# Three rounds of graph layers on one Trainium2 core: another order of sweeps, a fifth bank, splits lowered later, and three fp32r passes in rows that took fp32

## The chip, the cores and the metric

The kernel runs on one core of a Trainium2 chip. The metric is device time in microseconds (us) of one execution, the median over several. The engines are named as in the profile: PE is TensorE (PEld its weight load), DVE is VectorE, ACT is ScalarE, POOL is GpSimd and SP is SyncE, which here only starts transfers.

## The reference, cut to what matters

`adj` is 4096 x 4096, node features are 4096 x 128, and everything is fp32.

```python
def _mlp(x, W1, b1, W2, b2, W3, b3):        # a = leaky_relu, slope 0.01
    x = a(x @ W1 + b1)
    x = a(x @ W2 + b2)
    return a(x @ W3 + b3)

u = x
for _ in range(3):
    v = _mlp(adj @ u, uv_W1, uv_b1, uv_W2, uv_b2, uv_W3, uv_b3)
    u = _mlp(adj @ v, vu_W1, vu_b1, vu_W2, vu_b2, vu_W3, vu_b3)
x = layernorm(x + v)
x = layernorm(x + adj @ (x @ weight))
```

Only the v of the third round is used. So `adj` is multiplied six times, each time with the result of the time before: products 0 to 4 are followed by the three layers, product 4 also by the first normalization, and product 5 by the projection and the second normalization.

## The kernel before, in words

**Splitting.** A product is worked out in three passes of the type fp32r: a tile of `adj` is split into `high` (an ACT copy, L427) and `low` (raw minus `high`, a DVE subtraction, L551), and the operand into `p_high` and `p_low`. The passes are high by `p_low`, high by `p_high`, low by `p_high` (L771).

**Tiles and visits.** The 4096 rows are 8 chunks of 512. A tile holds 512 rows by 256 columns and is 0.5 MB; a chunk of columns is two tiles, loaded together by one transfer of 1 MB. A visit is one tile multiplied into one sum in PSUM: six matmuls. Each product has 128 visits, 768 in all. Where the operands allow, a tile once split is visited for product k and then for product k+1, before it is thrown away (`both`). There are 8 slots for split tiles (`SLOTS`) and four raw buffers of two tiles.

**Sweeps.** Product 0 with 56 visits of product 1 is the first sweep of 184 visits. Sweep k (1 to 4) has 128 visits: the rest of product k, and 56 of product k+1. The last sweep is the remaining 72 visits of product 5. In a sweep, "row r" means the r-th chunk in the sweep's order, which runs upwards and downwards in turn. Sweep k begins with the corner tiles of rows 1, 2, 3 and 0; then row 1's tiles of column 0; corner tiles of rows 4 to 6 as partial sums that are put aside ("more"); row 2's tiles for product k; row 1's tiles of column 0 for product k+1; row 2's tiles again for product k+1; and then rows 3 to 7 with each tile visited for both. In row 7, the last six tiles (`HELD`) are first all visited for product k and then all for k+1.

**Sums.** A sum lives in one of the banks `acc` of PSUM. Its goal says how it ends: "keep" is copied by ACT to `part`, "more" is added to `part` by DVE (`grow`, L577), "finish" is added to what is in `part` by DVE (`finish`, L585), "whole" is taken directly. The first matmul of a sum waits until the bank's sum before has been read (`wait_bank`).

**Chunks.** When a sum of product 0 to 4 is finished, its chunk goes through the layers: layers 1 and 2 on PE either as one fp32 matmul (L710, L721) or, where `halves` is true, as three fp32r passes (L689, L690, L692), for which ACT writes `h_high` and DVE `h_low` (L590, L595); then layer 3 (`layer_3`, L727, eight small matmuls), the bias addition on DVE (L600), the activation on ACT (L479, L481) and `p_low` on DVE (`lower_third`, L608). For product 4 the activation is followed by the sum with the residual and the statistics on DVE (`measure`, L621 to L628), the root on ACT (L485), the inverse on DVE (L635, L637), the normalization on ACT (L494), `p_high` on ACT (`raise_normed`, L502) and `p_low` on DVE (`lower_normed`, L643).

**The order by hand.** All queues are written out over one count n of visits. PE does visit n and, before it, what is due at n. ACT and DVE do at n what is due for chunks and sums, and then the splits that are due. A chunk starts at `start`, when its sum is finished, but not closer to the chunk before than `SPACING`, nor to the last but one than `TWO_APART`. Its layers stand 3, 6 and 8 visits later with three passes, and 3, 5 and 7 with fp32. The steps after the third layer stand 1 to 6 visits behind it. The split of tile t, on ACT and on DVE alike, is due at

```python
        def split_before(t):
            return max(0, plan.opening[t] - AHEAD, plan.closing[t - SLOTS] + 1 if t >= SLOTS else 0)
```

A transfer into a raw buffer waits until DVE has made `low` of both tiles that were in it (L389).

Of the kernel before, what the change touches and what calls it, by code (L numbers as in the profile page):

```python
# [12 lines left out]
D = 128  # L13
CHUNK = 512
CHUNKS = N // CHUNK
# [9 lines left out]
RAWS = 8  # L25
SLOTS = 8
AHEAD = 6
BANKS = 4
HELD = 6

X_PIECES = [1, 1, 2, 4]

# [16 lines left out]

PROJECT, LAST_MEASURE, LAST_ROOT, LAST_INVERT, LAST_NORMALIZE = 4, 5, 6, 7, 8  # L50

SPACING = [2] * NORMED + [4, 3]
BETWEEN = 14
TWO_APART = [10] * NORMED + [14]

WHOLE_ROWS = [0, 1, 2, 7]

@dataclass
# [35 lines left out]
class Plan:  # L95
# [54 lines left out]

    def sweep(self, k):
        rows = list(range(CHUNKS)) if k % 2 == 0 else list(range(CHUNKS))[::-1]
        opened = {}

        def corner(r, goal):
            opened[r] = self.open(k, rows[r], goal)
            self.one(rows[r], self.band([rows[r]]), opened[r])

        for r in range(1, OPENED + 1):
            corner(r, "finish")  # L160
        corner(0, "finish")
        self.one(rows[1], self.band(rows[:1]), opened[1])
        for r in range(OPENED + 1, CHUNKS - 1):
            corner(r, "more")
        made = self.one(rows[2], self.band(rows[:2]), opened[2])
        self.one(rows[1], self.band(rows[:1]), self.open(k + 1, rows[1], "keep"))
        second = self.open(k + 1, rows[2], "keep")
        for t in made:
            self.visit(t, second)
        for r in range(3, CHUNKS - 1):  # L170
            first = opened[r] if r <= OPENED else self.open(k, rows[r], "finish")
            self.both(rows[r], self.band(rows[:r]), first, self.open(k + 1, rows[r], "keep"), 0)
        first = self.open(k, rows[-1], "whole")
        self.one(rows[-1], self.band(rows[-1:]), first)
        self.both(rows[-1], self.band(rows[:-1]), first, self.open(k + 1, rows[-1], "keep"), HELD)

    def last_sweep(self):
        rows = list(range(CHUNKS))[::-1]
# [9 lines left out]
    def place_chunks(self):  # L188

        for i, s in enumerate(self.sums):  # L190
            s.opens = min(n for n, v in enumerate(self.visits) if v.total == i)
            s.closes = max(n for n, v in enumerate(self.visits) if v.total == i)
            s.read = s.closes + 1
        finished = [i for i, s in enumerate(self.sums) if s.goal in ("whole", "finish")]
        for i in sorted(finished, key=lambda i: self.sums[i].closes):
            s = self.sums[i]
            if self.chunks:
                apart = SPACING[s.product] if s.product == self.sums[self.chunks[-1].total].product else BETWEEN
                s.read = max(s.read, self.chunks[-1].start + apart)
            if len(self.chunks) > 1 and s.product < LAST:  # L200
                s.read = max(s.read, self.chunks[-2].start + TWO_APART[s.product])
            s.finished = len(self.chunks)
            row = s.chunk if s.product % 2 == 0 else CHUNKS - 1 - s.chunk
            halves = row not in WHOLE_ROWS or (s.product == 0 and row < CHUNKS - 1)
            self.chunks.append(Chunk(i, s.read, s.read + (LAYER_3 if halves else WHOLE_LAYER_3), halves))

    def place_parts(self):

        for s in self.sums:
            for before in self.sums:  # L210
                if (before.product, before.chunk, before.goal) == (s.product - 1, s.chunk, "finish") and s.goal == "keep":
                    s.read = max(s.read, before.read + 1)
                    s.follows = self.sums.index(before)
        for goal in ("whole", "finish", "keep", "more"):
            for nth, s in enumerate(sorted((s for s in self.sums if s.goal == goal), key=lambda s: s.read)):
                s.nth = nth
# [13 lines left out]
def gnn_kernel(nc, adj, x_nodes, weights, biases, spread, out):  # L230
# [4 lines left out]
    with ExitStack() as ctx:  # L235
# [3 lines left out]
        def psum(name, shape):  # L239
            return ctx.enter_context(nc.psum_tensor(name, shape, F32))  # L240
# [27 lines left out]

        acc = [psum(f"acc{i}", [D, CHUNK]) for i in range(BANKS)]
        layer = [psum(f"layer{i}", [D, CHUNK]) for i in range(2)]  # L270
        proj = [psum(f"proj{i}", [D, CHUNK]) for i in range(2)]

        x_loaded = [sem(f"x_loaded{i}") for i in range(len(X_PIECES))]
        consts_loaded = sem("consts_loaded")
# [86 lines left out]
            return max(0, plan.opening[t] - AHEAD, plan.closing[t - SLOTS] + 1 if t >= SLOTS else 0)  # L361

        split_at = [split_before(t) for t in range(len(tiles))]

        def made_by(product, chunk):

# [181 lines left out]
        def _(dve):  # L548
# [49 lines left out]
            def add_bias(i):  # L598
                dve.wait_ge(proj_done, i + 1)
                nc.vector.tensor_tensor(  # L600
                    h[i % 2][:].rearrange("p (j d) -> p j d", d=D), proj[i % 2][:].rearrange("p (j d) -> p j d", d=D),
                    b_spread[f"{way_of(i)}_b3"][:].unsqueeze(1).to_broadcast([D, IN_CHUNK, D]),
                    ALU.add).then_inc(biased, 1)

# [7 lines left out]
            def measure(i):  # L612

                if layered(i):
                    dve.wait_ge(third_ready, i + 1)
                    source = h[i % 2]
                else:
                    dve.wait_ge(proj_done, i + 1)
                    source = proj[i % 2]
                    dve.wait_ge(normed_ready, i - NORM)  # L620
                nc.vector.tensor_tensor(h[i % 2][:], source[:], resid[:, blocks_of(sum_of(i).chunk)],  # L621
                                        ALU.add).then_inc(x_added, 1)
                dve.wait_ge(x_added, i - NORM + 1)
                for j in range(IN_CHUNK):
                    nc.vector.bn_stats(stats[:, j, :], block_in(h[i % 2], j)).then_inc(stats_ready, 1)  # L625
                for j in range(IN_CHUNK):
                    dve.wait_ge(stats_ready, (i - NORM) * IN_CHUNK + j + 1)
                    done = nc.vector.bn_aggr(moments[:, j, :], stats[:, j, :])  # L628
                done.then_inc(moments_ready, 1)
# [17 lines left out]
            for n in range(END):  # L647
                if n == TILES - 1:
                    lower_weights()
                for i, chunk in enumerate(chunks):  # L650
                    if n == chunk.start and finishes(i):
                        finish(i)
                    if layered(i):
                        if n == chunk.start + LOWER_SUM and chunk.halves:
                            lower_sum(i)
                        if n == chunk.start + LOWER_FIRST and chunk.halves:
                            lower_first(i)
                        if n == chunk.third:
                            add_bias(i)
                    if plain(i) and n == chunk.third + P_LOWER:  # L660
                        lower_third(i)
                    if normed(i):
                        if n == chunk.third + MEASURE:
                            measure(i)
                        if n == chunk.third + INVERT:
                            invert(i)
                        if n == chunk.third + NORM_P_LOWER:
                            lower_normed(i)
                    if not layered(i):
                        if n == chunk.start + LAST_MEASURE:  # L670
                            measure(i)
                        if n == chunk.start + LAST_INVERT:
                            invert(i)
                for s in sums:
                    if s.goal == "more" and n == s.read:
                        grow(s)
                for t in range(len(tiles)):
                    if n == split_at[t]:
                        if t % IN_BAND == 0 and t // IN_BAND < CHUNKS:
                            lower_x(t // IN_BAND)  # L680
                        split(t)
# [3 lines left out]
        def _(pe):  # L685
# [38 lines left out]
            def turning(i, source, weight):  # L724

                for j in range(IN_CHUNK):
                    done = nc.tensor.matmul(block_in(proj[i % 2], j), block_in(source, j), weight[:], start=True,  # L727
                                            stop=True)
                done.then_inc(proj_done, 1)

            def layer_3(i):
                pe.wait_ge(second_ready, i + 1)
                if i >= 2:
                    pe.wait_ge(biased, i - 1)
                turning(i, h[i % 2], w[f"{way_of(i)}_W3"])

            def project(i):
                wait_sum(i)
                if i >= FINAL + 2:
                    pe.wait_ge(x_added, i - NORM - 1)  # L740
                else:
                    pe.wait_ge(biased, i - 1)
                turning(i, h[i % 2], w["gcn_W"])

            def wait_bank(before):
# [76 lines left out]
```

## Time and profile before

| | |
|---|---|
| median of 3 runs | 1225.14 us (1224.45 to 1227.73) |
| the profiled execution | 1227.23 us, span 1225.5 us |
| busy | PE 1173.3 us (96%), DVE 727.7 (59%), ACT 666.4 (54%) |
| read from HBM | 262.74 MB, mean 217 GB/s |
| mean granted clock of PE | 0.984 of full |

### The profile page before, as it was taken

How to read it: one execution, taken by the hardware profiler on the slowest of the kernel's cores; microseconds unless marked ns; L12 is line 12 of the kernel's file. 1: busy time of each engine (PE TensorE's matmuls, PEld its weight loads, DVE VectorE, ACT ScalarE, POOL GpSimd, SP SyncE). 2: the span in 40 equal slices, each digit the busy share in tenths (PEclk: the TensorE clock that was granted, in tenths of full speed). 3: DMA queues.
4: the chain of work that ended last, by engine and by line, in shares of the span. 5: the costliest groups of instructions: out<-in, count | busy, mean ns of one | idle time of the engine just before them, and what ended most of it. 6: DMA issues, size and time to landing. Idle time of an engine off the chain costs nothing. (4 is left out here: it accounts for less than half of the span.)

```text
span 1225.5 us, 13700 instructions
## 1 busy us (share of the span) xinstructions
PE 1173.3 (96%) x5198; PEld 956.0 (78%) x5198; DVE 727.7 (59%) x857; ACT 666.4 (54%) x837; POOL 10.6 (1%) x24
## 2 busy tenths in 40 slices
PE   5999999999999999999999999999977889999986
PEld 4788888888788888788888788888855778887875
DVE  5976555556555544745454854555653445559886
ACT  5876544446554544654444754445644345566774
POOL 2000000000000000000000000000000000000000
PEclk9999999999999999999999999999988889999999
DMA  9977665655545546744445844465542334558883
GB/s 355 384 287 275 237 231 207 239 206 215 198 172 210 188 162 231 274 162 179 175 187 194 309 173 168 172 240 206 208 171 103 138 138 171 207 206 312 324 312 150
DMA packets 37535, 265.72 MB, mean 217 GB/s; under 512 B 4432, under 2 KB 4432, under 8 KB 5600
## 3 DMA queue, kind: packets, MB, share of 16 engines
q1 hardware_dynamic: 36576, 262.68, 57.5%
q0 software_dynamic: 896, 2.17, 0.5%
q8 instruction: 43, 0.70, 0.2%
q14 instruction: 20, 0.16, 0.0%
HBM read 262.74 MB, written 2.10 MB: 216 GB/s over the span
## 5 line engine op out<-in xcount | busy, mean ns | idle before, releaser
L551 DVE TENSOR_TENSOR low<-raw,high 128x1024 fp32r<-128x1024 f32 x496 | 588.9, 1221 | 361.1 <-ACT high L427 360.9
L771 PE MATMUL acc<-high,p_low 128*128 128x512 f32 x1536 | 623.5, 406 | 40.1 <-DVE p_low L643 19.6
L771 PE MATMUL acc<-low,p_high 128*128 128x512 f32 x1536 | 604.3, 393 | 0.0
L771 PE MATMUL acc<-high,p_high 128*128 128x512 f32 x1536 | 604.0, 393 | 0.0
L427 ACT ACTIVATE high<-raw 128x1024 fp32r<-128x1024 f32 x496 | 494.9, 1049 | 58.6 <-PE acc L771 34.6
L771 PEld LDWEIGHTS acc<-high,p_low 128*128 128x128 f32 x1536 | 292.0, 190 | 113.1 <-DVE low L551 27.1
L771 PEld LDWEIGHTS acc<-high,p_high 128*128 128x128 f32 x1536 | 292.4, 190 | 66.0 <-issue 7.4
L771 PEld LDWEIGHTS acc<-low,p_high 128*128 128x128 f32 x1536 | 291.8, 190 | 62.9
L454 ACT ACTIVATE h_high<-h 128x512 fp32r<-128x512 f32 x16 | 10.1, 632 | 119.5 <-DVE h L585 119.5
L585 DVE TENSOR_TENSOR h<-acc,part 128x512 f32<-128x512 f32 x35 | 24.1, 688 | 74.9 <-PE acc L771 70.4
L479 ACT ACTIVATE p_high<-h 128x512 fp32r<-128x512 f32 x32 | 20.2, 632 | 65.1 <-DVE h L600 65.1
L469 ACT ACTIVATE h<-layer,b_uv_b 128x512 f32<-128x512 f32 x24 | 16.5, 688 | 38.9 <-PE layer L692 23.2
L509 ACT ACTIVATE h<-acc 128x512 f32<-128x512 f32 x6 | 3.6, 600 | 60.2 <-PE acc L771 60.2
L481 ACT ACTIVATE h<-h 128x512 f32<-128x512 f32 x40 | 24.8, 619 | 14.6 <-DVE h L600 14.6
L444 ACT ACTIVATE part<-acc 128x512 f32<-128x512 f32 x35 | 20.8, 595 | 18.0 <-PE acc L771 18.0
L727 PEld LDWEIGHTS proj<-w_uv_W,h 128*128 128x128 f32 x192 | 25.1, 191 | 2.0
L464 ACT ACTIVATE h<-layer,b_uv_b 128x512 f32<-128x512 f32 x24 | 16.4, 685 | 18.0 <-PE layer L710 18.0
L485 ACT ACTIVATE std<-moments,eps 128x4 f32<-128x4 f32 x16 | 4.8, 298 | 39.1 <-DVE moments L628 39.1
L727 PE MATMUL proj<-w_uv_W,h 128*128 128x128 f32 x192 | 25.3, 275 | 0.0
L469 ACT ACTIVATE h<-layer,b_vu_b 128x512 f32<-128x512 f32 x16 | 11.0, 688 | 25.0 <-PE layer L692 13.0
L608 DVE TENSOR_TENSOR p_low<-h,p_high 128x512 fp32r<-128x512 f32 x32 | 22.0, 687 | 3.8 <-ACT h L481 3.7
L454 ACT ACTIVATE h_high<-acc 128x512 fp32r<-128x512 f32 x7 | 4.2, 596 | 35.4 <-PE acc L771 35.4
(64 smaller groups left out, 372.5 us busy)
## 6 DMA issues: line engine op xcount, KB each, us to landing
raw<-adj_dram SPq DMA_DIRECT2D x248, 1024.0 KB, 4.9
out_dram<-part POOLq DMA_DIRECT2D x6, 256.0 KB, 4.5
resid<-x_dram SPq DMA_DIRECT2D x1, 1024.0 KB, 17.6
resid<-x_dram SPq DMA_DIRECT2D x2, 256.0 KB, 5.3
resid<-x_dram SPq DMA_DIRECT2D x1, 512.0 KB, 11.7
out_dram<-part SPq DMA_DIRECT2D x2, 256.0 KB, 2.0
w_uv_W<-uv_W_dram POOLq DMA_DIRECT2D x3, 64.0 KB, 7.8
w_vu_W<-vu_W_dram POOLq DMA_DIRECT2D x3, 64.0 KB, 7.8
```

Source lines behind the costliest of these rows:

```text
L427: nc.scalar.activation(high[t % SLOTS][:], raw_of(t), ACT.Copy).then_inc(high_ready, 1)
L444: nc.scalar.activation(part_of(s.chunk), acc[s.bank][:], ACT.Copy).then_inc(part_kept, 1)
L454: nc.scalar.activation(h_high[:], summed(i)[:], ACT.Copy).then_inc(sum_raised, 1)
L464: nc.scalar.activation(h[i % 2][:], layer[0][:], ACT.Prelu, bias=bias, alpha=SLOPE).then_inc(first_ready, 1)
L469: nc.scalar.activation(h[i % 2][:], layer[1][:], ACT.Prelu, bias=b[f"{way_of(i)}_b2"][:], alpha=SLOPE).then_inc(second_ready, 1)
L479: nc.scalar.activation(p_high[k % 2][:, blocks_of(c)], h[i % 2][:], ACT.Prelu, alpha=SLOPE).then_inc(p_high_ready, 1)
L481: nc.scalar.activation(h[i % 2][:], h[i % 2][:], ACT.Prelu, alpha=SLOPE).then_inc(third_ready, 1)
L551: nc.vector.tensor_tensor(low[t % SLOTS][:], raw_of(t), high[t % SLOTS][:].bitcast(F32), ALU.subtract).then_inc(low_ready, 1)
L585: nc.vector.tensor_tensor(h[i % 2][:], acc[s.bank][:], part_of(s.chunk), ALU.add).then_inc(total_ready, 1)
L608: nc.vector.tensor_tensor(p_low[k % 2][:, blocks_of(c)], h[i % 2][:], p_high[k % 2][:, blocks_of(c)].bitcast(F32), ALU.subtract).then_inc( ...
L727: done = nc.tensor.matmul(block_in(proj[i % 2], j), block_in(source, j), weight[:], start=True, stop=True)
L771: done = nc.tensor.matmul(bank[:], p[parity][:, at:at + D], a[slot][:, columns], start=(n == s.opens and j == 0 and m == 0), stop=(n == s. ...
```

## The change

- `sweep` is written anew. The partial corner sums of rows 4 to 6 stay where they are for products 1 to 3; row 3's two tiles of column 0 are taken before row 1's tiles of column 0 for product k+1, so that two more visits lie ahead of those, and are visited again behind row 2's. In sweep 4 the fillers are other tiles: row 5's corner, rows 6 and 7 with two columns each, and four tiles are loaded and split a second time at the end of rows 6 and 7. Row 7 of product 4 is a "finish" there.
- `HELD` goes from 6 to 8, `BANKS` from 4 to 5, and the second `proj` bank goes: a third layer waits for the bias addition of the chunk before, and a projection of the last product for the sum with the residual of the chunk before.
- `LAG = 2`: DVE's part of a split (`low`) is due two visits later than ACT's part.
- `SPACING` for product 4 goes from 4 to 2.
- `WHOLE_ROWS`: rows 2 and 7 no longer take fp32 layers but three passes; only rows 0 and 1 of a sweep do.
- `place_parts`: a "keep" copy waits for the finished sum that last read the same place in `part`.

```diff
+LAG = 2
-BANKS = 4
-HELD = 6
+BANKS = 5
+HELD = 8
-SPACING = [2] * NORMED + [4, 3]
+SPACING = [2] * LAST + [3]
-WHOLE_ROWS = [0, 1, 2, 7]
+WHOLE_ROWS = [0, 1]
...
     def sweep(self, k):
+        for r in range(OPENED + 1):
+            opened[r] = self.open(k, rows[r], "finish")
+        for r in [*range(1, OPENED + 1), 0]:
+            some(r, [r], opened[r])
+        some(1, [0], opened[1])
+        if k < NORMED:
+            fill = {4: [4], 5: [5], 6: [6]}
+        else:
+            fill = {5: [5], 6: [6, 5], 7: [7, 6]}
+        for r, places in fill.items():
+            some(r, places, self.open(k, rows[r], "more" if r < CHUNKS - 1 else "keep"))
+        of_2 = some(2, [0, 1], opened[2])
+        of_3 = some(3, [0], opened[3])
+        for r in (1, 2, 3):
+            kept[r] = self.open(k + 1, rows[r], "keep")
+        some(1, [0], kept[1])
+        for t in of_2:
+            self.visit(t, kept[2])
+        for t in of_3:
+            self.visit(t, kept[3])
+        self.both(rows[3], self.band(rows[1:3]), opened[3], kept[3], 0)
+        for r in range(OPENED + 1, CHUNKS):
+            first = self.open(k, rows[r], "finish" if r in fill or r < CHUNKS - 1 else "whole")
+            second = self.open(k + 1, rows[r], "keep")
+            if r not in fill:
+                some(r, [r], first)
+            alone = [i for i in fill.get(r, []) if i != r]
+            shared = [rows[i] for i in range(r) if i not in alone]
+            self.both(rows[r], self.band(shared), first, second, HELD if r == CHUNKS - 1 else 0)
+            some(r, alone, second)
...
-            halves = row not in WHOLE_ROWS or (s.product == 0 and row < CHUNKS - 1)
+            halves = s.product < LAST and (row not in WHOLE_ROWS or (s.product == 0 and row < CHUNKS - 1))
...
-        proj = [psum(f"proj{i}", [D, CHUNK]) for i in range(2)]
+        proj = psum("proj", [D, CHUNK])
...
+        lowered_at = [max(max(split_at[u], plan.opening[u] - AHEAD + LAG) for u in range(t + 1))
+                      for t in range(len(tiles))]
...
-                    if n == split_at[t]:
+                    if n == lowered_at[t]:
                         if t % IN_BAND == 0 and t // IN_BAND < CHUNKS:
                             lower_x(t // IN_BAND)
                         split(t)
...
             def layer_3(i):
                 pe.wait_ge(second_ready, i + 1)
-                if i >= 2:
-                    pe.wait_ge(biased, i - 1)
+                if i:
+                    pe.wait_ge(biased, i)
...
             def project(i):
                 wait_sum(i)
-                if i >= FINAL + 2:
-                    pe.wait_ge(x_added, i - NORM - 1)
+                if i > FINAL:
+                    pe.wait_ge(x_added, i - NORM)
                 else:
-                    pe.wait_ge(biased, i - 1)
+                    pe.wait_ge(biased, FINAL)
```

## Rows read from the trace of the kernel before

**Rows 1.** The page: busy time, and the granted clock in 40 slices
```profile
PE 1173.3 (96%) x5198; PEld 956.0 (78%) x5198; DVE 727.7 (59%) x857; ACT 666.4 (54%) x837; POOL 10.6 (1%) x24
...
PEclk9999999999999999999999999999988889999999
```

**Rows 2.** Busy time by window: sweep 2, sweep 4, the last sweep
```profile
core 0: us, PE busy (x) PEld busy (x) DVE busy (x) ACT busy (x) POOL busy (x), PEclk, DMA share, GB/s
...
484.28:678.60 194.32, 194.32 (x874) 158.85 (x873) 108.35 (x108) 100.13 (x123) 0.00 (x0) 1.00 0.54 201
...
872.92:1100.59 227.67, 205.25 (x873) 165.17 (x872) 123.33 (x185) 115.34 (x159) 0.00 (x0) 0.94 0.46 171
1100.59:1216.90 116.31, 109.13 (x497) 88.51 (x495) 99.09 (x164) 81.22 (x111) 3.26 (x6) 0.99 0.81 295
```

**Rows 3.** The chain that ended last: start us, us, what; three visits
```profile
962.93 4.09 PE acc L771 x18
```

**Rows 4.** PE's waits in the whole span, and one in the timeline
```profile
PE acc L771 <- DVE p_low L643: 19.6, 4, 5.6
...
PE acc L771 <- issue: 2.8, 1, 2.8
...
984.77 0.79 PE L771 MATMUL acc<-high,p_low 128*128 128x512 f32 x1 [5.23 <-DVE p_low L643]
```

**Rows 5.** Busy time by window: the five stretches at half clock in sweep 4
```profile
sum 27.22, PE 21.65 PEld 16.59 DVE 10.55 ACT 2.38 POOL 0.00; mean PE 4.33 PEld 3.32 DVE 2.11 ACT 0.48 POOL 0.00
```

**Rows 6.** The chain that ended last, from a third layer to its `p_low`
```profile
970.46 0.91 PE proj L727 x8
...
972.65 1.05 ACT high L427
...
973.73 1.23 DVE low L551
974.95 0.61 DVE h L621
...
975.59 0.87 DVE stats L625 x4
...
979.20 0.18 DVE rstd L635
...
980.00 1.25 ACT resid L494 x3
...
982.89 1.23 DVE low L551
984.11 0.61 DVE p_low L643
```

**Rows 7.** DVE's timeline: seven `low` back to back
```profile
844.61 8.03 DVE L551 TENSOR_TENSOR low<-raw,high 128x1024 fp32r<-128x1024 f32 x7
```

**Rows 8.** Waits in the last sweep, and PE's timeline in it
```profile
DVE low L551 <- ACT high L427: 13.5, 17, 2.2
...
PE acc L771 <- DVE low L551: 5.1, 4, 2.2
...
PE proj L727 <- DVE h L585: 2.0, 2, 1.2
...
1168.73 0.50 PE L771 MATMUL acc<-high,p_low 128*128 128x512 f32 x1 [0.84 <-DVE low L551]
1169.07 0.39 PE L771 MATMUL acc<-high,p_high 128*128 128x512 f32 x1
```

**Rows 9.** The chain that ended last: an fp32 layer; one of three passes
```profile
1094.87 0.86 PE layer L710 x2
...
967.02 0.23 PE layer L689
```

**Rows 10.** PE's timeline: the first chunk's first layer
```profile
46.11 0.50 PE L692 MATMUL layer<-h_low,w_high_uv_W 128*128 128x512 f32 x1 [2.14 <-DVE h_low L590]
```

**Rows 11.** Busy time by window, in the first sweep
```profile
41.00:54.00 13.00, 10.37 (x38) 7.75 (x37) 11.43 (x15) 9.81 (x15) 0.00 (x0) 0.87 1.01 399
```

**Rows 12.** Loads of `adj` in 1100 to 1210 us, issue to landing
```profile
DMA to landing us min/median/max: 4.7/6.2/8.0
```

More of the change, by code:

```diff
@@ L152, in sweep @@
         rows = list(range(CHUNKS)) if k % 2 == 0 else list(range(CHUNKS))[::-1]
[L153 to L174, printed above, removed]
@@ L175, in sweep, with some @@
-        self.both(rows[-1], self.band(rows[:-1]), first, self.open(k + 1, rows[-1], "keep"), HELD)
+        opened, kept = {}, {}
+        def some(r, places, total):
+            return self.one(rows[r], self.band([rows[i] for i in places]), total)
+        for r in range(OPENED + 1):
[7 more added lines that the diff above has]
+            fill = {5: [5], 6: [6, 5], 7: [7, 6]}
@@ L209, in place_parts @@
         for s in self.sums:
-            for before in self.sums:
-                if (before.product, before.chunk, before.goal) == (s.product - 1, s.chunk, "finish") and s.goal == "keep":
+            if s.goal == "keep":
+                read = [b for b in self.sums if b.goal == "finish" and b.closes < s.closes
+                        and b.chunk % (CHUNKS - 1) == s.chunk % (CHUNKS - 1)]
+                if read:
+                    before = max(read, key=lambda b: b.closes)
                     s.read = max(s.read, before.read + 1)
@@ L600, in add_bias @@
                 nc.vector.tensor_tensor(
-                    h[i % 2][:].rearrange("p (j d) -> p j d", d=D), proj[i % 2][:].rearrange("p (j d) -> p j d", d=D),
+                    h[i % 2][:].rearrange("p (j d) -> p j d", d=D), proj[:].rearrange("p (j d) -> p j d", d=D),
                     b_spread[f"{way_of(i)}_b3"][:].unsqueeze(1).to_broadcast([D, IN_CHUNK, D]),
@@ L618, in measure @@
                     dve.wait_ge(proj_done, i + 1)
-                    source = proj[i % 2]
+                    source = proj
                     dve.wait_ge(normed_ready, i - NORM)
@@ L726, in turning @@
                 for j in range(IN_CHUNK):
-                    done = nc.tensor.matmul(block_in(proj[i % 2], j), block_in(source, j), weight[:], start=True,
+                    done = nc.tensor.matmul(block_in(proj, j), block_in(source, j), weight[:], start=True,
                                             stop=True)
```

## The prediction

> **What bounds the kernel now.** I read the busy shares first: PE is busy 96% of the span and DVE and ACT under 60% [rows 1]. So two things can move the end: less work on PE, or fewer stretches in which PE stands still or is granted half its clock. The slices show where the second kind lies. PE and its clock read 9 throughout, except in slices 30 to 33, around 900 to 1000 us.
>
> Next I cut the span at the sweeps. Every sweep from 1 on is 128 visits; I took the start of each from the start of its first matmul, counting six matmuls to a visit. Sweep 2 lasts 194.32 us with PE busy all of it, and sweeps 1 and 3 the same to the hundredth. Sweep 4 has the same number of visits and layers and lasts 227.67 us, and the last sweep's 72 visits take 116.31 us [rows 2].
> - One visit is six matmuls: three visits take 4.09 us, so 1.365 us each, 0.2275 us a matmul [rows 3].
> - Sweep 4 is 33.35 us longer than sweep 2. PE idle accounts for 227.67 - 205.25 = 22.4 us of that [rows 2]: one wait of 2.8 us and four of 19.6 together, up to 5.6 us each [rows 4]. The other 10.9 us is the half clock behind each of them: the five stretches at a granted clock of about 0.5 hold 21.65 us of PE work [rows 5], which at full clock is half of it.
> - The four name the low half of the operand of the next product (`p_low`, made by `lower_normed`). The one put down to "issue" comes at position 12, before the matmul that opens chunk 5's sum: it is the wait for a bank of PSUM, which `finish` of chunk 1 releases.
>
> The chain of waits shows what one of these consists of. The third layer of a chunk ends at 971.37 and its `p_low` at 984.72 us, 13.35 us later [rows 6]. Only about 7 us of it is the chunk's own work. The rest is three pairs of `high` on ACT (1.05 us) and `low` on DVE (1.23 us), that is 3 x 2.28 = 6.8 us, splits of later tiles that stand in both queues between the chunk's steps, each `low` just behind its own `high`. The third layer stands six visits before the first use of its result: 8.2 us. 13.35 - 8.2 = 5.2 us, the idle that the row at 984.77 shows [rows 4].
>
> **Sweep 4 after the change.** I write positions as visits from the sweep's start, T for the position of a third layer, and count from the diff. For product 4, old order against new:
> - Chunk 0: T 15 in both; first used at 20, now at 26.
> - Chunk 1: `SPACING` 4 to 2 brings T from 19 to 17; first used at 24, now at 30.
> - Chunk 2 (row 2): closes at 23 instead of 19, three passes instead of fp32, T 29 to 32; first used at 35, now at 39. Seven visits instead of six.
> - Chunk 3: T 45 to 49, used at 51, now 57. Eight instead of six.
> - Chunk 4: T 67, used at 77. Chunks 5 and 6 have 13 and 19 visits. Chunk 7: T at 126, used at 140, before 129 and 140.
>
> `LAG` changes the chain itself. A `low` stands two positions later in DVE's queue, so its `high` is normally done and DVE doesn't wait for it, and the last `low` before `p_low` no longer waits for a `high` that stands behind the normalization. With bias 0.7, `low` 1.15 (seven back to back took 8.03) [rows 7], sum and statistics 1.9, `low` 1.15, inverse 0.4, normalization 1.3, raising 0.6 and `p_low` 0.6 [rows 6] that is 7.8 us, 8.4 with the gaps between engines. For chunk 2 there is also a `high` before the normalization, so 9.2. Against seven visits, 9.6 us, and eight, 10.9 us: no idle at chunk 3, and 0 to 1 us at chunk 2. Chunks 0 and 1 have 15.0 and 17.7 us, but lie in 28 consecutive visits that each need a new tile. From the third layer of chunk 0 to visit 25, DVE has 7 x 1.15 + two statistics (3.8) + four additions and subtractions (2.4) + inverses (0.7) = 15.0 us and once waits for ACT (0.6), against ten visits and one third layer (0.9) on PE, 14.6: 1 us of idle. The same again at visit 27 gives 1.5. The bank wait of 2.83 goes: the fifth bank takes the first filler, and each later bank has been read four visits before it is opened, not two; chunk 1 is finished at 10, not 12. In sum I leave 3.5 us of idle in sweep 4, in pieces under 2 us. A wait of 0.84 us in the last sweep is followed by a matmul at the full pace, 0.39 us; the 5.23 us one is not, 0.79 us [rows 4, 8]. Gain 33.35 - 3.5 = **29.9**, bounds 20 (chains as long as today, below) and 33.3.
>
> **Passes.** Row 2 of products 1 to 4, row 7 of products 0 to 3 and row 7 of product 4 go from fp32 to three passes: 9 chunks, 18 layers. An fp32 layer takes PE 0.86 us, three passes 3 x 0.23 = 0.69 [rows 9]. 18 x 0.17 = **3.1 us**. It adds 18 subtractions of some 0.65 us on DVE and as many copies on ACT, less the `take` of row 7, hidden since DVE idles 44% of sweep 2 [rows 2]. Each such T comes one visit later: chunk 2 of products 1 to 3 has seven visits to its use, row 7 six (it closes two earlier), for a plain chain of four steps of some 0.65 us, the size of the addition at 974.95 [rows 6]. The Trainium skill, FP8 and Floating Point Precision, TensorE Precision Notes, counts four passes for true fp32; at 0.2275 us a pass that would be 0.91 against 0.69, and the gain 3.9. The row decides; the gap is 0.8 us.
>
> **Last sweep.** 72 visits (98.3) and eight blocks of 0.9 us before the last chunk's make 105.5 us; it takes 116.3, so 10.8 are lost: waits for `low` of 5.1 in all, for the finished sum 2.0 before projections [rows 8], half clock after the longest, 2.2 us (1.7), the rest in short ones. DVE idles 13.5 us here waiting for `high` while ACT waits for statistics [rows 8]: the same interlock, which `LAG` undoes, and chunk 7's chain comes three visits earlier. DVE's own work is 72 x 1.15 + 8 x 2.8 = 105 us less a lead of about four tiles (4.6): just under PE's. A lead shorter by two tiles and the single `proj` bank (the next projection waits for the sum of the chunk before) leave something, I take 3 us, bounds 0 and 8. Gain 10.8 - 3 = **7.8**.
>
> **First sweep.** The first chunk's layer waits 2.14 us for `h_low` [rows 10], and the clock halves behind it: 0.87 over 13 us [rows 11] is 3.4 us at half, 1.6 lost. With the lag one tile's `low` fewer stands before it, so it comes 1.1 us sooner. But DMA is at 1.01 of its share at 399 GB/s there [rows 11], so more can't be had. **1.5**, bounds 0 and 3.
>
> **At no cost.** Four more tiles (two loads of 1 MB, 500 splits instead of 496): ACT and DVE have the room. Single `proj` in sweeps: a third layer waits for the bias addition of the chunk before, due two visits (2.7 us) earlier and some 0.65 us long. `HELD` 8: the eight second visits need no new tile; the next ones are split at six visits ahead as before. The changed `follows` only orders copies.
>
> **Sum.** 29.9 + 3.1 + 7.8 + 1.5 = 42.3 us. The profiled execution: 1227.23 - 42.3 = 1184.9. It was 2.1 above the median of the runs, 1225.14, so I predict **1183**.
>
> **Rivals.**
> 1. *The normalized chains stay 13.4 us long* (ACT's order, not DVE's, holds them). Then chunk 2 idles 13.4 - 9.6 = 3.8 and chunk 3 2.5, each with some 2 us of half clock behind it [rows 5]: 10.3 us. The last sweep keeps its interlocks, and gains only the 2.2 us wait and its half clock by the earlier chunk 7: 3.9 us more. With the 1 us that I have at chunk 2 taken out that is 13 us, 1196. For it: ACT's `high` stands before the normalization in both orders. Against: `low` before `p_low` plainly waits for a later `high`. 0.14.
> 2. *DVE becomes the bound where every visit needs a tile* (0 to 27 of sweep 4, last sweep): two statistics close together, with less lead. Stalls over 2 us there, and the clock falls: 6 to 10 us more, 1191. 0.12.
> 3. *Loads starve, slower.* A later `low` frees `raw` later, so a load begins up to two visits (2.7 us) later. In single-visit stretches a ring of four 1 MB buffers must turn in eight visits, 10.9 us; a turn is landing + 1.05 + 2 x 1.2 = landing + 3.45. It decides at a landing time of 7.5 us; the median is 6.2 in the last sweep, 8.0 at most [rows 12]. Single visits number 16 + 3 x 24 + 28 + 72 = 188, some 23 turns; to end slower by 0.3% they must cost 46 us, 2 us a turn, landings of 9.5 us: 1229 or more. 0.03; a mild form of it is in rival 2. The Trainium skill, DMA: Bandwidth & Descriptors, Rules for kernel authors, wants a DMA issued early and waited for late, which the lag goes against; its fit (2.0 us + bytes over 436 GB/s) would give 4.4 us for these loads, the least in that stretch is 4.7.
> 4. *It does not do what it says*: a new wait (the single `proj`, a bank, a later third layer of row 2 or 7) in each of sweeps 1 to 4 gives the gain back, 10 us a sweep: 1225, no change. PE idles nowhere in sweep 2 now [rows 2] and every slack I count is larger than the chain. 0.02.
>
> Mine has 0.69. Its own range is 1176 (no idle left in sweep 4 nor in the last) to 1189. For eight in ten I take 1175 to 1197, which takes in rivals 1 and 2 mostly. About 0.3% (3.7 us) can be told from no change. Faster 0.95, same 0.02, slower 0.03.
>
> **What would show it.** Sweep 4 near 197 us, with no wait for `p_low` over 2 us and a granted clock of 1.00 there; from third layer to `p_low` 8 to 9 us; waits of DVE's `low` for `high` down by far more than the gain; sweeps 2 and 3 at 193.6 us; last sweep 107 to 111. The prediction is wrong if a wait for `low` or a load opens in the first 28 visits of a sweep, or if chunk 2's seven visits don't do.

## The result, and the profile after

The changed kernel takes 1181.74 us (median of 4 runs, 1181.15 to 1182.57) against 1224.8 us for the kernel before, timed beside it: ratio 0.9646, 95% interval 0.9627 to 0.9666, faster by 3.5%. The prediction was 1183 us, range 1175 to 1197. Its profiled execution took 1181.15 us with a span of 1179.2 us.

The page of the changed kernel, busy time and granted clock [rows 1]:

```profile
PE 1154.8 (98%) x5216; PEld 950.7 (81%) x5216; DVE 739.8 (63%) x879; ACT 680.8 (58%) x855; POOL 10.5 (1%) x24
...
PEclk9999999999999999999999999999999999999999
```

The dip in slices 30 to 33 is gone. Busy time by window, cut again at the starts of sweep 2, sweep 4 and the last sweep [rows 2]:

```profile
core 0: us, PE busy (x) PEld busy (x) DVE busy (x) ACT busy (x) POOL busy (x), PEclk, DMA share, GB/s
...
481.67:675.19 193.52, 193.52 (x880) 159.61 (x878) 110.54 (x112) 102.20 (x126) 0.00 (x0) 1.00 0.54 201
...
868.71:1064.30 195.59, 194.18 (x880) 159.47 (x879) 129.26 (x194) 121.90 (x166) 0.00 (x0) 1.00 0.57 210
1064.30:1170.57 106.27, 105.38 (x489) 86.93 (x487) 98.87 (x165) 80.83 (x108) 3.25 (x6) 1.00 0.84 324
```

The span fell by 46.3 us: sweep 4 by 227.67 - 195.59 = 32.1, the last sweep by 10.0, sweeps 1 to 3 by 0.80 each (2.4), the first sweep by 1.6 and its start by 0.25. What PE still waits for, over the whole span [rows 4, 8, 10]:

```profile
PE acc L790 <- DVE low L570: 14.2, 6, 10.0
PE layer L708 <- ACT h_high L473: 1.6, 2, 1.4
PE layer L711 <- DVE h_low L609: 1.0, 1, 1.0
PE proj L746 <- ACT h L528: 0.7, 1, 0.7
```

10.0 us of the first row is the start of the kernel. Another 3.4 us of it lies in the next 18 us, in the first visits of the first sweep; the kernel before waited 2.3 us for `low` there. No wait for `p_low` is left. DVE's timeline shows why, for chunk 3 of product 4, whose third layer ends at 947.63 us (lines are 19 further down than before) [rows 6]:

```profile
947.67 0.69 DVE L619 TENSOR_TENSOR h<-proj,b_uv_b 128x512 f32<-128x512 f32 x1 [3.81 <-PE proj L746]
948.28 1.22 DVE L570 TENSOR_TENSOR low<-raw,high 128x1024 fp32r<-128x1024 f32 x1
949.41 0.68 DVE L640 TENSOR_TENSOR h<-h,resid 128x512 f32<-128x512 f32 x1
950.12 0.87 DVE L644 BATCH_NORM_STATS2 stats<-h 128x6 f32<-128x128 f32 x4
950.91 0.37 DVE L647 BATCH_NORM_AGGREGATE moments<-stats 128x2 f32<-128x6 f32 x4
951.19 1.20 DVE L570 TENSOR_TENSOR low<-raw,high 128x1024 fp32r<-128x1024 f32 x1
952.30 0.17 DVE L654 RECIPROCAL rstd<-std 128x4 f32<-128x4 f32 x1
...
952.60 1.23 DVE L570 TENSOR_TENSOR low<-raw,high 128x1024 fp32r<-128x1024 f32 x1
955.05 0.69 DVE L662 TENSOR_TENSOR p_low<-resid,p_high 128x512 fp32r<-128x512 f32 x1 [1.23 <-ACT p_high L521]
```

The same three `low` stand between the same steps, but none has a wait in front of it (the brackets are on the bias and on `p_low` only). `p_low` ends at 955.74, 8.1 us after the third layer, where it took 13.35. The last `low` now runs while ACT normalizes. The chains of chunks 2 to 5 were 13.4 us and are 8.1. Those of chunks 0 and 1, where every visit needs a tile, are still 13.7 and 12.6 us (12.9 and 17.5 before): PE doesn't wait for them because their first use comes later in the new order.

### The profile page after: what moved, and what is told of

Its sections match the earlier page's. It is cut to its first block, busy times and chain, and to the rows that moved or that the text cites. A ratio compares the mean times of both kernels' runs of the same rounds, so it can differ in the third digit from the quotient of the medians.

```text
span 1179.2 us, 13786 instructions
## 1 busy us (share of the span) xinstructions
PE 1154.8 (98%) x5216; PEld 950.7 (81%) x5216; DVE 739.8 (63%) x879; ACT 680.8 (58%) x855; POOL 10.5 (1%) x24
## 3 DMA queue, kind: packets, MB, share of 16 engines
q0 software_dynamic: 896, 2.17, 0.5%
## 4 chain that ended last, share of the span: by engine, by line
PE 91%; DVE 5%; DMA 3%; ACT 1%; issue 1%; ACTq 0%; SPq 0%; DVEq 0%
PE acc L790 82%; PE proj L746 3%; DVE low L570 3%; DMA raw<-adj_dram 3%; PE layer L711 1%; PE layer L708 1%; PE layer L709 1%; PE layer L740 1%; PE layer L729 1%; DVE stats L644 0%; ACT part L513 0%; DVE h L640 0%; ACT high L446 0%; DVE h L604 0%; DVE moments L647 0%
## 5 line engine op out<-in xcount | busy, mean ns | idle before, releaser
L790 PE MATMUL acc<-high,p_low 128*128 128x512 f32 x1536 | 609.3, 397 | 14.2 <-DVE low L570 14.2
L446 ACT ACTIVATE high<-raw 128x1024 fp32r<-128x1024 f32 x500 | 500.2, 1050 | 80.9 <-DMA raw<-adj_dram 40.8
L614 DVE TENSOR_TENSOR h_low<-h,h_high 128x512 fp32r<-128x512 f32 x32 | 22.1, 692 | 70.2 <-ACT h L483 70.2
L619 DVE TENSOR_TENSOR h<-proj,b_uv_b 128x512 f32<-128x512 f32 x24 | 16.6, 690 | 63.9 <-PE proj L746 63.9
L609 DVE TENSOR_TENSOR h_low<-acc,h_high 128x512 fp32r<-128x512 f32 x11 | 7.6, 691 | 77.8 <-ACT h_high L473 77.8
L619 DVE TENSOR_TENSOR h<-proj,b_vu_b 128x512 f32<-128x512 f32 x16 | 11.1, 691 | 41.6 <-PE proj L746 41.6
L488 ACT ACTIVATE h<-layer,b_uv_b 128x512 f32<-128x512 f32 x24 | 16.5, 688 | 30.3 <-PE layer L711 24.3
L481 ACT ACTIVATE h_high<-layer,b_uv_b 128x512 fp32r<-128x512 f32 x20 | 13.7, 686 | 34.1 <-PE layer L711 34.1
```

The costliest lines, as they stand in the source:

```text
L446: nc.scalar.activation(high[t % SLOTS][:], raw_of(t), ACT.Copy).then_inc(high_ready, 1)
L488: nc.scalar.activation(h[i % 2][:], layer[1][:], ACT.Prelu, bias=b[f"{way_of(i)}_b2"][:], alpha=SLOPE).then_inc(second_ready, 1)
L614: nc.vector.tensor_tensor(h_low[:], h[i % 2][:], h_high[:].bitcast(F32), ALU.subtract).then_inc(first_lowered, 1)
L619: nc.vector.tensor_tensor(h[i % 2][:].rearrange("p (j d) -> p j d", d=D), proj[:].rearrange("p (j d) -> p j d", d=D), b_spread[f"{way_of(i ...
L790: done = nc.tensor.matmul(bank[:], p[parity][:, at:at + D], a[slot][:, columns], start=(n == s.opens and j == 0 and m == 0), stop=(n == s. ...
```

## The experiments

Each was timed in rounds with the kernel before. Times are medians; where two variants differ by a few us, the intervals of their ratios to the kernel before (about 0.0015 to 0.002 each way, 2 us) say what that is worth. Lengths of sweeps and of waits are those of one profiled execution each.

**The kernel before with the lag alone.**

```diff
+LAG = 2
+        lowered_at = [max(max(split_at[u], plan.opening[u] - AHEAD + LAG) for u in range(t + 1)) ...]
-                    if n == split_at[t]:      # DVE
+                    if n == lowered_at[t]:
```

> The kernel before with the lag of two visits on DVE's part of a split alone; order, banks and fp32 rows as before. If the interlock of low behind its own high makes the chains long, the way from a third layer's end to p_low falls from 13.35 us to some 8.1 us (as in the changed kernel), chunks 2 and 3, with six visits (8.2 us), idle no more, chunks 0 and 1 (five visits) idle some 2 to 4 us each: sweep 4 falls from 227.7 us to 205 to 212, the last sweep by some 6 us, the time to 1195 to 1202 us. If the new order is what counts and the lag only moves instructions, sweep 4 stays within 5 us of 227.7 and the time above 1217 us.

Measured: 1189.56 us, ratio 0.9697 (0.9682 to 0.9711), below the range I gave. Its page has the granted clock at 0.999. PE's timeline, the waits of sweep 4:

```profile
889.35 0.47 PE L774 MATMUL acc<-high,p_low 128*128 128x512 f32 x1 [0.90 <-issue]
906.05 0.47 PE L774 MATMUL acc<-high,p_low 128*128 128x512 f32 x1 [1.03 <-DVE p_low L646]
913.59 0.50 PE L774 MATMUL acc<-high,p_low 128*128 128x512 f32 x1 [1.84 <-DVE p_low L646]
```

In the old order, the two waits of 5.23 us are gone, and those at chunks 0 and 1 are down from 3.51 and 5.61 to 1.03 and 1.84. Sweep 4 takes 199.5 us, the last sweep 107.7. One line of the plan carries 36 of the 43 us. I had given chunks 0 and 1 more idle than they have, and half clock behind it. These waits did not bring any: the granted clock over sweep 4 is 1.00.

**The changed kernel without the lag.** (`LAG = 0`)

> The changed kernel with a lag of 0, all else as changed. If the interlock makes the chains long, they are 13.4 us again: chunk 2 idles 13.4 - 9.6 = 3.8 us, chunk 3 2.5 us, each with about 2 us of half clock behind it, and the last sweep loses 4 to 7 us more: 1192 to 1198 us. If the order alone brought the gain, within 2 us of 1181.7 us.

Measured: 1200.69 us, ratio 0.979 (0.9775 to 0.9805), above my range. So all the rest of the change without the lag (order, banks, held tiles, spacing, passes) is worth 25 us, and the lag on top of it 19. How the 25 us divide among these parts was not measured. The chain that ended last, from chunk 3's third layer to `p_low`:

```profile
952.01 0.90 PE proj L746 x8
...
954.20 1.05 ACT high L446
955.27 1.23 DVE low L570
...
958.53 1.05 ACT high L446
...
963.37 1.05 ACT high L446
964.44 1.23 DVE low L570
965.67 0.61 DVE p_low L662
```

It is the interlock again, 13.4 us from 952.91. Chunk 3 idles 2.52 us as expected; chunk 2 only 0.80. Four `low` stand in its chain, but only the last of them waits for its `high`, 2.19 us, so the chain is 10.3 us. Its first layer waits 3.0 us for `h_high`. Sweep 4 takes 204.96 us. More than I expected is lost in the last sweep, 115.2 us. Waits there:

```profile
PE proj L746 <- DVE h L640: 5.6, 3, 2.2
...
PE proj L746 <- DVE h L604: 1.7, 2, 1.1
```

**Without the lag, and two `proj` banks** (`BANKS = 4`, and bank and waits of `proj` as before the change).

> The changed kernel with a lag of 0, four banks for sums and the two proj banks and their waits as before the change. With lag 0 and one proj bank PE waited 5.6 us for the sum with the residual, in front of projections. If that is the price of the single proj bank, it goes: 1195 us. If the fifth bank for sums is worth more than that, or DVE is late anyhow and the wait only moves to low, 1200 or above.

Measured: 1201.09 us, ratio 0.9798 (0.9779 to 0.9817). The 5.6 us are gone, and 3.5 us of waits for `low` and 1.0 more for the finished sum stand in their place; the last sweep is 113.5 us instead of 115.2, and the time the same. (3.4 us at half clock fell into the last sweep of the one profiled execution and into the first sweep of the other.) Most of the wait on the single bank only showed that DVE was late. The exchange of a bank for sums against one for `proj` is worth nothing at a lag of 0; the two were not taken apart.

**The changed kernel with the old order of sweeps 1 to 4.**

> The changed kernel with the old function for sweeps 1 to 4, but the lag, five banks, eight held tiles, spacing 2 and the three-pass rows of the change. With chains of 8.1 us: chunk 2 has five visits (6.8 us) and idles 1.3 us, chunk 3 six (8.2 us) and idles nothing, chunks 0 and 1 five and seven visits in the stretch where each visit needs a tile (13.7 us was measured there for chunk 0): 3 to 7 us of idle with half clock. 1187 to 1195 us. If lag and banks alone carry the gain and the order is worth nothing: 1182 us.

Measured: 1185.21 us, ratio 0.9664 (0.9646 to 0.9682), below my range. Waits for `p_low` of 2.54 (chunk 0) and 1.35 us (chunk 2, the amount worked out); sweep 4 takes 199.88 us, 4.3 more than in the new order. So once the lag is there, the order is worth 4.3 us of sweep 4 and 3.5 us by the medians, which lies inside the intervals, for all that it is most of the diff.

**The kernel before with three passes in rows 2 and 7.**

> The kernel before with three passes in rows 2 and 7 alone (layers of product 5, which has none, are kept out of that flag as in the change). By the rows of the changed kernel 18 layers x 0.20 us = 3.6 us less on PE; by my sum 3.1. Against it stands one visit more of delay for chunk 2 of product 4, which PE waits for already: 1.4 us and perhaps some half clock. Sweeps 2 and 3: 193.5 us. Time 1222 to 1223 us. If the later third layers cost more than the passes give (rival), 1225 or above.

Measured: 1222.07 us, ratio 0.9958 (0.9941 to 0.9975). One visit more of delay made a chain late even in sweeps 1 to 3, where before nothing waited: 0.20 us for `p_low` of row 7, at position 6 of each (and of sweep 4). Sweep 2 takes 194.02 us, not 193.5:

```profile
487.02:681.04 194.02, 193.82 (x877) 159.43 (x876) 111.02 (x113) 101.80 (x125) 0.00 (x0) 1.00 0.55 201
```

In sweep 4 the price that I expected for chunk 2 did not come, and the reverse did. Sweep 4 takes 221.55 us, 6.1 less than before, and chunk 2's wait is this in place of 5.23 us:

```profile
951.34 0.50 PE L771 MATMUL acc<-high,p_low 128*128 128x512 f32 x1 [1.35 <-DVE p_low L643]
```

Its third layer stands one visit later, at T 30 in place of 29, and its chain is 8.1 us long, with no lag at all: no `low` in it waits for its `high`. Chunk 3, whose place is unchanged, still has 13.4 us. So the interlock hangs on where the chunk's steps fall among the splits, and moving the chunk by one visit can undo it as moving `low` does. The time lies in the forecast range all the same, by luck: in the profiled execution the first sweep was 2.6 us longer, by waits and half clock at the first chunk's layer, which this edit doesn't touch.

**The changed kernel with fp32 in rows 2 and 7.**

> The changed kernel with fp32 layers in rows 2 and 7 as before. By the sweeps (194.32 to 193.52 us for 4 layers) an fp32 layer costs 0.20 us more than three passes: 18 x 0.20 = 3.6 us, 1185.3 us. By the single row of the chain of before (0.86 against 0.69) 3.1 us, 1184.8. If three passes cost as much in ACT and DVE work as they give on PE: 1182.

Measured: 1183.96 us, ratio 0.9666 (0.9652 to 0.9681): by the medians 2.2 us of the change are the passes, at the edge of the intervals. Sweeps 1 to 3 take 194.32 us again, 0.80 more each. In sweep 4 the passes give nothing: 195.38 us with fp32, 195.59 with three passes. PE has 0.8 us less work there, but chunk 2's first layer waits 1.41 us for `h_high`, with fp32 0.7 us for the sum itself.

**Fp32 in row 0 alone.** (`WHOLE_ROWS = [0]`)

> The changed kernel with row 1 of products 1 to 4 in three passes too, so that only row 0 takes fp32. 8 layers x 0.20 = 1.6 us less on PE; each third layer of row 1 comes one visit later, with 8 visits to its use in sweeps 1 to 3 and 12 in sweep 4. 1180.1 us if every chain is short enough; if chunk 1 of sweep 4, in the stretch where DVE is full, becomes late, 1181 to 1184.

Measured: 1179.83 us, ratio 0.9632 (0.9618 to 0.9647). The sweeps take 193.18 us (0.34 less for two layers, 0.17 each), sweep 4 194.80.

**Lag 1, and lag 4.**

> The changed kernel with a lag of 1. Tiles of rows visited twice are due every two visits, so a low moved by one visit still stands, mostly, between the same steps of the chunk, but its high is now one step earlier: the interlock should be gone where every visit needs a tile, and mostly where every second does. Between the 1181.7 us of lag 2 and the 1200.7 us of lag 0: I expect 1183 to 1188 us, nearer to 2. If only the lead of low before its visit counts, and not its distance from its high, the time rises in a line: 1191 us.

Measured: 1179.94 us, ratio 0.9635 (0.9619 to 0.9651), no worse than a lag of 2 and 1.8 us better by the medians. Chunk 3's chain is 8.12 us with lag 1, 8.11 with lag 2 and 13.37 with lag 0. So the distance of `low` from its `high` counts and one step of it is enough. Neither of my two readings expected a gain.

> The changed kernel with a lag of 4: low is due two visits (2.7 us) before it is needed, and raw buffers are freed two visits later still. The sum and statistics of a chunk alone take DVE 1.8 us, and two low 2.3 us, so PE waits for low in each of the stretches with one tile a visit: 1186 to 1195 us, by waits for low. If loads are what a lag costs (rival 3 of the prediction), the waits of high for DMA rise well above the 40.8 us of the changed kernel and landing times pass 7.5 us. If the lag has no price, 1182 us.

Measured: 1200.73 us, ratio 0.9808 (0.9789 to 0.9828), above my range. The last sweep takes 119.2 us with a granted clock of 0.97, by waits for `low` of 10.6 us. Part of the chain that ended last, in front of one of 3.69 us:

```profile
1098.84 6.93 DMA raw<-adj_dram
...
1106.76 1.04 ACT high L446
1107.80 1.55 ACT part L513 x4
...
1109.45 0.70 DVE h L640
1110.17 0.87 DVE stats L644 x4
1111.05 0.28 DVE moments L647 x3
1111.33 1.12 DVE low L570
...
1112.49 3.78 PE acc L790 x8
```

Both causes are in it: the load, issued when a late `low` freed its buffer, holds up `high` on ACT, behind it the normalization, behind that the next statistics on DVE, and behind them the `low` that PE needs. Waits of `high` for loads rise to 97.4 us from 40.8. But the loads of the last sweep are no slower: from 1070 to 1170 us the median landing is 5.4 us, 5.6 with lag 2, both at most 7.7, and never the 9.5 of my third rival. Loads begin later.

**The bank wait.** (`BANKS = 4`, `SPACING` of product 4 back to 4)

> The changed kernel with four banks for sums and the spacing of 4 for product 4. Chunk 1 is then finished at position 12 of sweep 4, where the filler of row 6 opens the bank it held: no slack. The kernel before lost 2.83 us and half clock there, with lag alone 0.90 us. 1182.5 to 1185 us, with a wait at position 12; if that wait was not for the bank, 1181.7.

Measured: 1182.04 us, ratio 0.9641 (0.9622 to 0.9659), just below my range. The wait is back where it was, at position 12, but with 0.90 us as in the kernel before with the lag, not 2.83. It is for a bank, though not for the one that I named in the prediction and in this expectation. The plan of both kernels with four banks opens the sum at position 12 in the bank of the filler before it, which closed at position 11, and `grow` reads that one. Chunk 1's bank is opened at 14 or 16. In the kernel before, DVE's `grow` ends just before PE goes on:

```profile
893.28 0.68 DVE L577 TENSOR_TENSOR part<-acc,part 128x512 f32<-128x512 f32 x1
...
894.07 0.76 PE L771 MATMUL acc<-high,p_low 128*128 128x512 f32 x1 [2.83 <-issue]
```

There `grow` stands behind `finish` of chunk 1 (0.68 us) and behind a `low` that itself waited 1.21 us for its `high`. With the lag it starts 0.1 us after the filler's last matmul has ended, and 0.90 us is what is left. The fifth bank takes this away. What the spacing gives by itself was not measured, and the time of both together is that of the changed kernel.

**Both small gains together**, and the same place for `low` by another way (`AHEAD = 7`, `LAG = 2`).

> The changed kernel with a lag of 1 and fp32 layers in row 0 alone. Each alone gave 1.8 us and 1.9 us. If they are independent (passes on PE against waits of the last sweep and of sweep 4) 1178.1 us; if both took away the same waits, 1179.8.

> The changed kernel with fp32 in row 0 alone, splits due seven visits ahead on ACT and, with the lag of 2, five on DVE: DVE's place is that of lag 1, with two visits between high and low. If what the lag of 2 costs is the lead of low before its visit (and with it the release of raw buffers), this does as well as lag 1 with row 0: 1178 us. If ACT then stands waiting for a slot or a load in front of the chunk's own steps, 1180 to 1186.

Measured: 1180.04 us (ratio 0.9625, 0.9604 to 0.9647) and 1180.11 us (0.9639, 0.9617 to 0.9661). In the traces the gains are added (spans of 1176.3 us against 1177.9 with row 0 alone and 1178.1 with lag 1), in the timed runs they can't be told from either alone: those of the first lay between 1178.06 and 1182.48. Lag 1 or row 0 alone, about 1180 us, is as good a version as I can show; it is 1.8 us below the changed kernel, at the edge of what is measured. The second, meant to tell what the gain of lag 1 comes from, can't tell it for the same reason.

## Why the prediction was right

- *What bounds, and the interlock*: right, and shown from both sides. With the lag the chain of chunk 3 is 8.1 us (forecast 8.4), without it 13.4 in either order. Chunk 2's, forecast 9.2, is 8.1 too. Rival 1, that ACT's order holds the chain, falls with that. The reading of the bank wait was wrong: `grow` of the filler releases it, not `finish` of chunk 1. The 2.83 us go all the same.
- *Sweep 4*: forecast 197 us, measured 195.59. I had a gain of 29.9 us plus 0.7 for passes, and 32.1 came. The term that was mis-sized is the idle left, 3.5 us: it is 1.4. (Of the 10.9 us that I called half clock, 10.1 are: the five stretches at 0.50 hold 20.1 us of PE work.) The wait for `low` around visit 25 did not come. `p_low` of chunk 0 took 13.7 us of the 15.0 it had, and DVE kept ahead of PE to the end of that stretch, so rival 2 did not come about. What came is a wait of the first layer of chunk 2 for `h_high`, behind `finish` on a busy DVE, which I had not listed.
- *The parts don't add*: I booked sweep 4's gain to order and lag together, which was right for the sum. Taken singly they are substitutes: lag alone 36 us, all the rest alone 25, both 43. That is so in sweep 4, where the lag alone gives 28.2 us, the rest alone 22.7 and both 32.1: either shorter chains or more visits before the first use do for most of the waits. In the last sweep the lag gives nearly all, 8.6 us of 10.0.
- *Passes*: forecast 3.1 us. An fp32 layer costs 0.17 to 0.20 us more than three passes, so PE has 3.1 to 3.6 us less to do; undone alone it is 2.2 by the medians, 2.7 between the profiled executions, because three passes also put a longer chain of ACT and DVE in front of the layer, and where DVE is full, that is waited for. "Hidden since DVE idles 44%" was read from sweep 2 and used for sweep 4. My row of 0.86 gave 0.17. The four passes of the Trainium skill, FP8 and Floating Point Precision, TensorE Precision Notes, would by my estimate cost 0.2275 more for the fourth. The sweeps lie between the two and decide neither way.
- *Last sweep*: forecast a gain of 7.8, measured 10.0, of which 0.9 is chunk 7's third layer, that moved into sweep 4 and that I had not moved in the sum. The mis-sized term is the residue: I had 3, and it is 106.27 less 104.6 of work, 1.7 us, of which waits for `low` are 0.8. (The wait of 0.7 before the last projection lies behind this window, and was there before.)
- *First sweep*: 1.5 forecast, 1.6 measured. The layer's wait for `h_low` is 1.0 us, down from 2.14, and the clock stays up. That the sizes agree is luck in part. With a lag of 0 the same wait of 2.14 us was followed by no half clock, and that first sweep took 278.9 us against 279.7 before and 278.2 after. And waits for `low` at its start, the sign that I had named for being wrong, did grow, by 1.1 us.
- *The level*: the profiled executions differ by 46.1 us where I had 42.3, the medians by 43.1. The profiled execution of before lay 2.4 us above its median and that of after 0.6 below. Some 3 us of my agreement is that I took the difference off the median, which is luck. By the profiled executions the sum is 4 us short.
- *Rival 3, loads*: not at a lag of 2, real at 4, by loads that begin later. The rule of the Trainium skill (DMA: Bandwidth & Descriptors, Rules for kernel authors), to issue a DMA early and wait for it late, points the same way, and the traces agree: waits of `high` for loads were 22.6 us at lag 0, 29.1 at lag 1, 40.8 at lag 2 and 97.4 at lag 4. (The fit that the prediction took from this page is given there for transfers issued from GpSimd; these loads are issued from SP.)

## What to carry to other kernels

Where two in-order engines hand work to each other and both also serve a latency-bound chain, don't put the consumer's half of background work at the same place as the producer's half. One step between them took 5 us out of a chain of 13, and so did one step of the chain itself in one chunk. More than is needed eats lead: lag 2 is no faster than lag 1, and from lag 2 to lag 4 all 19 us were lost again. And look for the shortest edit first: ask of each chain both how long it is and how much work stands before its first use, since mending either makes the other worth little.

## What was not expected of the hardware

Waits of PE up to 1.84 us in sweep 4 of the kernel with the lag alone left the granted clock of that sweep at 1.00, the full 2.4 GHz. One of 2.17 us in the last sweep of the kernel before was not so cheap, as PE's timeline there shows:

```profile
1125.62 0.73 PE L771 MATMUL acc<-high,p_low 128*128 128x512 f32 x1 [2.17 <-DVE low L551]
1126.15 0.63 PE L771 MATMUL acc<-high,p_high 128*128 128x512 f32 x1
```

0.63 us is a matmul at 1.2 GHz, where 0.39 us is one at 2.4; the granted clock is 0.50 from 1125.66 to 1129.07 us. But the length of a wait does not decide it. With a lag of 1, a wait of 1.92 us near the start was followed by 3.4 us at half clock, and with a lag of 4 one of 2.55 us by none:

```profile
20.27 0.50 PE L790 MATMUL acc<-high,p_low 128*128 128x512 f32 x1 [1.92 <-DVE low L570]
...
21.39 0.63 PE L790 MATMUL acc<-high,p_high 128*128 128x512 f32 x1
```

```profile
1135.88 0.50 PE L790 MATMUL acc<-high,p_low 128*128 128x512 f32 x1 [2.55 <-DVE low L570]
1136.21 0.40 PE L790 MATMUL acc<-high,p_high 128*128 128x512 f32 x1
```

What decides is not shown here. What the clock cost is: up to PE's last matmul the profile before has seven stretches at half clock, 34.1 us together with 27.0 us of PE work in them, and that after has none. At full clock that work takes half as long, so 13.5 of the 46 us that the span fell are clock that came back with the waits gone.
